# Gated linear attention in fp32 instead of three split passes, with its decay windows folded into zeros and a new order of steps

## The chip, the cores and the metric

One Trainium2 chip, one of its cores. The metric is the time of the whole kernel in device microseconds; lower is better. Engines: TensorE (PE, with its weight loads as PEld), VectorE (DVE), ScalarE (ACT), GpSimd (POOL), SyncE (SP).

## What is computed

Input x is 16 sequences of 256 tokens with 256 features, fp32. Four blocks follow each other, each with a residual: causal softmax attention with 16 heads, a gated FFN whose weights come from splines, gated linear attention, and the same FFN again. The change touches the third:

```python
q = silu(x @ Wq.T) * K ** -0.5            # K = 16, x is the layer-normed input
k = sigmoid(x @ Wk.T)
g = log_sigmoid(-k)
S = exp(g_t)[:, None] * S + k_t[:, None] * v_t[None, :]   # v = x, for each token t
o_t = q_t @ S
go = o @ Wog.T + x @ Wig.T
out = rms_norm(o) * g_weight * go * sigmoid(go)
```

## The kernel before

X holds all 4096 tokens in SBUF as 32 tiles of 128 tokens. The stages run one behind the other: attention with one sequence per period (until about 380 us), FFN (eight pairs of sequences, to about 574 us), gated linear attention (one sequence n per period, to about 775 us), FFN. All instructions and semaphores are written by hand; each engine runs its own list in order, and the order inside a period of the linear attention stands in the `period` functions (TensorE L1172, ScalarE L1504, VectorE L1875, GpSimd L720).

The scan over tokens is turned into products. Decays of a sequence are cumulated within windows, q is multiplied by the cumulated decay from a reference token and k by that to it, `g_products` (L1122) multiplies k by q over 112 rows (seven groups of 16 features, each with its window), `g_masked` (L1848) sets the future to zero, and `g_output` (L1154) multiplies the result by the values. `g_values` (L1132) has already multiplied x by Wog, so that o and o @ Wog.T come out of one accumulation, onto which `g_gate_in` (L1143) has put x @ Wig.T.

Precision: TensorE runs its products in fp32r. Each operand is split into a high part (ScalarE copies it to an fp32r tile, names with `_hi`) and a low part (VectorE or GpSimd subtracts the high part from the original, `_lo`), and `mm3` (L404 to L408) adds three passes. So the trace has all such products on L406, L407 and L408; tiles tell them apart: `wqk` projections, `wog` values, `wig` gate, `am` output, `qk` products.

ScalarE: `g_norm` (L1440, normalised input of n+2), `g_high_turned` (L1432), `g_activate` (L1449: tanh, silu, tanh, k, decay), `g_high_qk` (L1464), `g_high_am` (L1469), `g_high_x` and `g_high_values` (L1438, L1474), `g_squares` (L1485), `g_gate` (L1491), `g_normalise` (L1498). VectorE: `g_scans` (L1832, L1833: forward and backward cumulated products), `g_decayed` (L1838 reciprocal, L1840, L1842), the low parts (L1825, L1846, L1857, L1861), `g_stats` (L1813 to L1820), `g_mean_square` (L1867). GpSimd: `g_windows` (L685 to L693: q, k and decays times their windows), `g_low_x` (L678), small powers (L672, L698), `g_residual` (L702, L706, L710).

Many work tiles lie in one tensor, so the trace names them all `spline`.

At the start of the kernel the weights are turned and split: high parts on ScalarE (L1234, L1239), low parts on VectorE (L1587, L1595); GpSimd builds spline factors (L593 to L605) once the second sequence is normalised (L1581, L610).

## Time and profile before

| | |
|---|---|
| median of 3 runs | 972.94 us (972.71 to 973.38) |
| profiled execution, whole | 969.64 us |
| its span, first to last instruction | 967.9 us |
| busy TensorE, weight loads | 840.5 us (87%), 721.2 (75%) |
| busy VectorE, ScalarE, GpSimd | 690.2 (71%), 544.0 (56%), 402.8 (42%) |
| mean granted TensorE clock | 0.951 of 2.4 GHz |

The page divides the span into 40 slices of 24.2 us and gives the busy share in tenths. A timeline row reads: start in us, duration in us, engine, line, operation, output <- inputs, shapes, count, and in brackets how long the engine stood idle before and whom it waited for. Starts of successive matmuls give their spacing; durations contain the pipeline and overlap. A group row reads: line, engine, operation, names, shapes, count | busy us, mean ns | idle before, with releasers.

### The profile page before, as it was taken

What the parts mean: (1) busy time and instruction counts of PE and PEld (TensorE: products, weight loads), DVE (VectorE), ACT (ScalarE), POOL (GpSimd) and SP (SyncE); (2) the same over time, 40 slices, a digit from 0 to 9 for tenths busy, and PEclk for the clock granted to TensorE, in tenths of its full rate; (3) what the DMA queues carried; (4) which work ended last, traced back from release to release, by engine and by line L of the source; (5) the groups of instructions that cost most, each with busy time, mean ns of one, the idle gap of its engine ahead of it and who ended that gap; (6) DMA issues with size and microseconds to landing.
All of it is one profiled execution on the core that took longest, in us unless ns stands there. A gap on an engine that the chain in (4) does not pass through costs nothing.

```text
span 967.9 us, 21849 instructions
## 1 busy us (share of the span) xinstructions
PE 840.5 (87%) x7444; PEld 721.2 (75%) x7444; DVE 690.2 (71%) x1317; ACT 544.0 (56%) x1064; POOL 402.8 (42%) x465
## 2 busy tenths in 40 slices
PE   4599899999999977899999997877777569999997
PEld 4477677777777755788888887776676558888887
DVE  7567777777778763677776668888889536776765
ACT  3156455554555544666666655666665346666664
POOL 3922223222232242222223327899998543233220
PEclk9689999999999997999999998899999779999999
DMA  5946756667566530000000000000000000000001
GB/s 178 118 77 89 133 82 97 90 96 96 84 95 83 84 63 19 17 1 1 0 0 2 1 1 1 1 0 0 0 0 1 1 1 23 24 22 22 22 24 44
DMA packets 33752, 41.00 MB, mean 42 GB/s; under 512 B 4319, under 2 KB 25216, under 8 KB 33648
## 3 DMA queue, kind: packets, MB, share of 16 engines
q1 hardware_dynamic: 33690, 40.20, 25.0%
q8 instruction: 36, 0.59, 0.3%
q14 instruction: 26, 0.21, 0.1%
HBM read 9.25 MB, written 5.24 MB: 15 GB/s over the span
## 4 chain that ended last, share of the span: by engine, by line
PE 37%; DVE 26%; ACT 14%; issue 12%; POOL 4%; SPq 2%; DMA 2%; DVEq 1%; ACTq 1%; POOLq 0%
DVE inter L1771 6%; PE bank L406 5%; PE pair_a L840 5%; PE bank L408 4%; PE bank L407 4%; ACT stk L1389 4%; ACT gact L1394 4%; PE bank L854 3%; PE bank L1040 3%; PE pair_b L809 3%; DVE spline L1838 3%; DVE am_lo L1857 2%; DVE in_lo L1776 2%; DVE st L1745 2%; PE bank L867 2%
## 5 line engine op out<-in xcount | busy, mean ns | idle before, releaser
L583 POOL TENSOR_SCALAR_AFFINE_SELECT prob<-prob 128x512 f32<-128x512 f32 x128 | 82.0, 641 | 213.7 <-ACT prob L1265 213.7
L1265 ACT ACTIVATE prob<-pair_a 128x768 f32<-128x768 f32 x128 | 103.6, 809 | 96.1 <-PE pair_a L840 95.0
L1776 DVE TENSOR_TENSOR in_lo<-inter,in_hi 128x512 fp32r<-128x512 f32 x128 | 98.8, 772 | 78.7 <-ACT in_hi L1402 78.1
L406 PE MATMUL bank<-wd_hi,in_hi 128*128 128x256 f32 x512 | 147.4, 288 | 8.1 <-DVE X L1782 6.6
L408 PE MATMUL bank<-wd_hi,in_lo 128*128 128x256 f32 x512 | 142.9, 279 | 0.0
L407 PE MATMUL bank<-wd_lo,in_hi 128*128 128x256 f32 x512 | 142.6, 279 | 0.0
L1402 ACT ACTIVATE in_hi<-inter 128x512 fp32r<-128x512 f32 x128 | 80.9, 632 | 95.1 <-DVE inter L1771 95.1
L1618 DVE TENSOR_REDUCE mx<-pair_b 128x6 f32<-128x768 f32 x124 | 118.1, 952 | 18.6 <-PE pair_b L821 16.9
L1771 DVE TENSOR_TENSOR inter<-gact,pair_b 128x512 f32<-128x512 f32 x128 | 87.6, 684 | 49.6 <-ACT gact L1394 43.7
L406 PEld LDWEIGHTS bank<-wd_hi,in_hi 128*128 128x128 f32 x512 | 96.7, 189 | 16.3 <-issue 5.8
L407 PEld LDWEIGHTS bank<-wd_lo,in_hi 128*128 128x128 f32 x512 | 97.1, 190 | 3.6
L408 PEld LDWEIGHTS bank<-wd_hi,in_lo 128*128 128x128 f32 x512 | 96.7, 189 | 0.0
L1050 PE MATMUL bank<-ident,xe 128*126 128x128 f32 x512 | 82.8, 286 | 12.5 <-POOL xe L654 7.6
L1389 ACT ACTIVATE stk<-bank 126x512 fp32r<-126x512 f32 x128 | 75.0, 586 | 18.2 <-PE bank L1050 18.2
L646 POOL COPY xe<-xr 128x448 f32<-128x448 f32 x32 | 24.7, 771 | 138.9 <-ACT xe L1371 138.9
L1394 ACT ACTIVATE gact<-pair_a 128x512 f32<-128x512 f32 x128 | 75.9, 593 | 0.0
L1050 PEld LDWEIGHTS bank<-ident,xe 128*126 128x126 f32 x512 | 59.3, 145 | 22.2 <-ACT stk L1389 11.6
L840 PE MATMUL pair_a<-stack 50*128 50x256 f32 x512 | 65.9, 336 | 10.7 <-DMA stack<-mrow 7.6
L840 PEld LDWEIGHTS pair_a<-stack 50*128 50x128 f32 x512 | 39.3, 190 | 34.6 <-issue 18.3
L1076 PE MATMUL pair_a<-stk,cst 126*128 126x512 f32 x128 | 63.0, 492 | 0.5 <-ACT stk L1389 0.5
L809 PE MATMUL pair_b<-stack 48*128 48x256 f32 x496 | 54.2, 297 | 5.0 <-DVE stage L1609 3.6
L1079 PE MATMUL pair_b<-stk,cst 126*128 126x512 f32 x128 | 51.7, 404 | 0.0
(242 smaller groups left out, 2340.8 us busy)
## 6 DMA issues: line engine op xcount, KB each, us to landing
stack<-stage SPq DMA_DIRECT2D x192, 128.0 KB, 4.7
result<-X SPq DMA_DIRECT2D x8, 512.0 KB, 2.9
X<-in_attn_a_x SPq DMA_DIRECT2D x14, 256.0 KB, 5.0
stack<-mrow SPq DMA_DIRECT2D x128, 4.0 KB
wdx<-spline SPq DMA_DIRECT2D x1, 1024.0 KB
wd_lo<-wdx SPq DMA_DIRECT2D x16, 64.0 KB
spline<-factor_basis SPq DMA_DIRECT2D x1, 1008.0 KB, 6.8
win<-decay_windows SPq DMA_DIRECT2D x1, 672.0 KB, 7.5
```

What stands on the lines that cost most here:

```text
L406: pe.matmul(dst, l_hi, r_hi, start=first, stop=False)
L407: pe.matmul(dst, l_hi, r_lo, start=False, stop=False)
L408: return pe.matmul(dst, l_lo, r_hi, start=False, stop=last)
L809: pe.matmul(dst[:, n, at_col:at_col + S], stack[rows, u, h, p % PR, 0, P * t:P * t + P], stack[rows, u, h, p % PR, 1, :], start=(t == 1), ...
L840: i = pe.matmul(pair_a[:, n, at_col:at_col + S], stack[rows, u, h, p % PR, 1, P * t:P * t + P], stack[rows, u, h, p % PR, 0, :], start=Tru ...
L1050: i = pe.transpose(bank_t[0:NFX, P * t:P * t + P], xe[:, u, t, m].rearrange("p c f -> p (c f)").bitcast(F32), ident[:, :])
L1265: act.activation(prob[:, p % 4], pair_a[:, :, P:4 * P], ACT.Exp, scale=DK ** -0.5).then_inc(a_e, 1)
L1389: act.activation(stk[:, m % 2, :], bank_t[0:NFX, :], ACT.Copy).then_inc(f_.st, 1)
L1394: act.activation(gact[:, m % 2, :], pair_a[:, m % 2, :], ACT.Silu).then_inc(f_.si, 1)
L1618: dve.tensor_reduce(mx[:, h, :, p % PR, :], src[:, :, 0:3 * P].rearrange("p n (t k) -> p n t k", t=3), AX.X, ALU.max).then_inc(a_mx, 1)
L1771: dve.tensor_tensor(inter[:, m % 2, :], gact[:, m % 2, :], pair_b[:, m % 2, :], ALU.mult).then_inc(f_.up, 1)
L1776: dve.tensor_tensor(in_lo[:, m % LAG, :], inter[:, m % 2, :], in_hi[:, m % LAG, :].bitcast(F32), ALU.subtract).then_inc(f_.il, 1)
```

## The change

All products of the linear attention are single fp32 matmuls on unsplit tiles; the high copies stay as plain fp32 copies (ScalarE), the low parts are gone. `g_high_qk`, `g_high_am`, `g_low_qk`, `g_low_am`, `g_low_values`, `g_low_turned`, `g_low_x` and `g_windows` are gone. There are five groups of 16 rows instead of seven, in 112 rows with two gaps that are zero: three cross groups (rows 0 to 47) and two near groups (64 and 96), each for one half of every 128 tokens. Windows are bounded by zeros that GpSimd sets once in `dec` and `fk`; the decay is written in three pieces. The products skip the block above the diagonal. q, k and decays have two buffers. On TensorE the projections of n+1 move behind output, gate and turn, the values of n+1 behind the products of n; on ScalarE the activations of n+1 move from the third place to nearly the last; on VectorE the statistics move ahead of the scans.

```diff
-NG = 7
-GR = NG * KG
+GROUPS = (0, 16, 32, 64, 96)
+CROSS = 48
+NEAR = (64, 96)
+GR = 112
+AM = 3 * P
...
+def decay_starts():
+
+    w = np.zeros((GR, 2, S), np.float32)
+    for g, ref in ((0, 64), (1, 192), (2, 128)):
         r = slice(KG * g, KG * g + KG)
-        run[r] = 1.0
...
+        w[r, 0, ref] = 1.0
+        w[r, 1, ref - 1] = 1.0
+    for h in range(2):
+        w[NEAR[h]:NEAR[h] + KG, 0, 64 * h::P] = GROW
...
-        wog = sb("wog_hi", [P, CT, D], F32R), sb("wog_lo", [P, CT, D], F32R)
-        wig = sb("wig_hi", [P, CT, D], F32R), sb("wig_lo", [P, CT, D], F32R)
-        wqk_hi = sb("wqk_hi", [P, 2, CT, GR], F32R)
-        wqk_lo = sb("wqk_lo", [P, 2, CT, GR], F32R)
+        wog = sb("wog", [P, CT, D], F32)
+        wig = sb("wig", [P, CT, D], F32)
+        wqk = sb("wqk", [P, 2, CT, GR], F32)
...
-        qs, kt, ks, dt, dec, qwn, kwn, dq, dk, fq, fk = (gwork(1, GR)[:, 0] for _ in range(11))
+        am = am.rearrange("p t k -> p (t k)")[:, 0:AM]
+        qs, ks, dec = (gwork(2, GR) for _ in range(3))
+        kt, dt, fq, fk = (gwork(1, GR)[:, 0] for _ in range(4))
...
-            def g_low_x(n, u):
...
             def g_project(n, u):
 
-                pe.wait_ge(g_.xl, upto(g_.xl, n, 1))
+                pe.wait_ge(g_.xh, upto(g_.xh, n, 1))
                 pe.wait_ge(g_.qs, upto(g_.qs, n - 1, 1))
                 pe.wait_ge(g_.kt, upto(g_.kt, n - 1, 1))
                 for w in range(2):
                     for c in range(CT):
-                        i = mm3(pe, bank_p[0:GR, S * w:S * w + S], wqk_hi[:, w, c, :], wqk_lo[:, w, c, :],
-                                gT_hi[:, u, c, :], gT_lo[:, u, c, :], c == 0, c == CT - 1)
+                        i = pe.matmul(bank_p[0:GR, S * w:S * w + S], wqk[:, w, c, :], gT[:, u, c, :], start=c == 0,
+                                      stop=c == CT - 1)
                 i.then_inc(g_.qk, 1)
...
             def g_products(n):
 
-                pe.wait_ge(g_.qkl, upto(g_.qkl, n, 1))
+                pe.wait_ge(g_.kd, upto(g_.kd, n, 1))
+                pe.wait_ge(g_.qd, upto(g_.qd, n, 1))
                 pe.wait_ge(g_.am, upto(g_.am, n - 1, 1))
-                for t in range(TB):
-                    keys = slice(P * t, P * t + P)
-                    i = mm3(pe, pair_a[:, 0, S * t:S * t + S], qk_hi[:, 1, keys], qk_lo[:, 1, keys],
-                            qk_hi[:, 0, :], qk_lo[:, 0, :], True, True)
+                for at, rows, k, q in ((0, GR, 0, 0), (P, CROSS, 0, 1), (2 * P, GR, 1, 1)):
+                    k, q = slice(P * k, P * k + P), slice(P * q, P * q + P)
+                    i = pe.matmul(pair_a[:, 0, at:at + P], qk[0:rows, 1, k], qk[0:rows, 0, q], start=True, stop=True)
                 i.then_inc(g_.ap, 1)
...
             def g_values(n, u):
 
-                pe.wait_ge(g_.xl, upto(g_.xl, n, 1))
-                pe.wait_ge(g_.wl, upto(g_.wl, n - 1, 1))
+                pe.wait_ge(g_.xh, upto(g_.xh, n, 1))
+                pe.wait_ge(g_.wh, upto(g_.wh, n - 1, 1))
                 for t in range(TB):
                     for c in range(CT):
                         tok = slice(P * t, P * t + P)
-                        i = mm3(pe, pair_a[:, 1, D * t:D * t + D], gT_hi[:, u, c, tok], gT_lo[:, u, c, tok],
-                                wog[0][:, c, :], wog[1][:, c, :], c == 0, c == CT - 1)
+                        i = pe.matmul(pair_a[:, 1, D * t:D * t + D], gT[:, u, c, tok], wog[:, c, :], start=c == 0,
+                                      stop=c == CT - 1)
                 i.then_inc(g_.xw, 1)
...
             def g_output(n, u):
 
-                pe.wait_ge(g_.gl, upto(g_.gl, n, 1))
-                pe.wait_ge(g_.wl, upto(g_.wl, n, 1))
-                pe.wait_ge(g_.aml, upto(g_.aml, n, 1))
+                pe.wait_ge(g_.gh, upto(g_.gh, n, 1))
+                pe.wait_ge(g_.wh, upto(g_.wh, n, 1))
+                pe.wait_ge(g_.am, upto(g_.am, n, 1))
                 for q in range(TB):
-                    tok = slice(P * q, P * q + P)
                     for part in range(2):
                         cols = slice(D * part, D * part + D)
                         for t in range(q + 1):
-                            i = mm3(pe, out_bank(u, q)[:, cols], am_hi[:, t, tok], am_lo[:, t, tok],
-                                    val_hi[:, u, t, cols], val_lo[:, u, t, cols], False, part == 1 and t == q)
+                            tok = slice(P * (q + t), P * (q + t) + P)
+                            i = pe.matmul(out_bank(u, q)[:, cols], am[:, tok], val[:, u, t, cols], start=False,
+                                          stop=part == 1 and t == q)
                     i.then_inc(g_.o, 1)
...
                 pe.wait_ge(f_.res, upto(f_.res, PAIRS - 1, 2))
 
                 def period(n, u, prev2=True, prev=True, cur=True, nxt=True, nxt2=True, nxt3=True):
-                    if nxt:
-                        g_project(n + 1, 1 - u)
-                        g_values(n + 1, 1 - u)
                     if not cur:
                         f2_turn(0, 0, 0, bank_t)
                         f2_turn(0, 0, 1, bank_p)
...
                         g_gate_in(n, u)
                     if nxt2:
                         g_turn(n + 2, u)
+                    if nxt:
+                        g_project(n + 1, 1 - u)
                     if cur:
                         g_products(n)
+                    if nxt:
+                        g_values(n + 1, 1 - u)
 
                 run_gla(pe, period)
...
-            def g_activate(n):
+            def g_activate(n, u):
 
                 act.wait_ge(g_.qk, upto(g_.qk, n, 1))
-                act.wait_ge(g_.w, upto(g_.w, n - 1, 4))
+                act.wait_ge(g_.kd, upto(g_.kd, n - 2, 1))
                 act.activation(kt, bank_p[0:GR, S:2 * S], ACT.Tanh, scale=0.5).then_inc(g_.kt, 1)
-                act.activation(qs, bank_p[0:GR, 0:S], ACT.Silu).then_inc(g_.qs, 1)
+                act.activation(qs[:, u], bank_p[0:GR, 0:S], ACT.Silu).then_inc(g_.qs, 1)
                 act.wait_ge(g_.kt, upto(g_.kt, n, 1))
                 act.activation(dt, kt, ACT.Tanh, bias=quarter[0:GR, :], scale=0.25).then_inc(g_.dt, 1)
-                act.activation(ks, kt, ACT.Copy, bias=0.5, scale=0.5).then_inc(g_.ks, 1)
+                act.activation(ks[:, u], kt, ACT.Copy, bias=0.5 * KG ** -0.5, scale=0.5 * KG ** -0.5).then_inc(g_.ks, 1)
                 act.wait_ge(g_.dt, upto(g_.dt, n, 1))
-                act.activation(dec, dt, ACT.Copy, bias=0.5, scale=-0.5).then_inc(g_.de, 1)
...
+                for rows, cut in (((0, 32), P), ((32, CROSS), 0), ((NEAR[0], GR), 64)):
+                    to, of = dec[rows[0]:rows[1], u], dt[rows[0]:rows[1]]
+                    if cut:
+                        to, of = (v.rearrange("p (w s) -> p w s", s=cut)[:, :, 1:] for v in (to, of))
+                    i = act.activation(to, of, ACT.Copy, bias=0.5, scale=-0.5)
+                i.then_inc(g_.de, 1)
...
-                    if prev:
-                        g_high_am(n - 1)
                     if prev2:
                         g_normalise(n - 2, u)
                     if not cur:
...
                         f2_store_turned(0, bank_t)
                     if nxt2:
                         g_norm(n + 2, u)
-                    if nxt:
-                        g_activate(n + 1)
-                    if cur:
-                        g_high_qk(n)
                     if prev:
                         g_squares(n - 1, 1 - u)
-                    if nxt:
-                        g_high_x(n + 1, 1 - u)
-                        g_high_values(n + 1, 1 - u)
                     if nxt2:
                         g_high_turned(n + 2, u)
                     if prev:
                         g_gate(n - 1, 1 - u)
+                    if nxt:
+                        g_high_x(n + 1, 1 - u)
+                        g_activate(n + 1, 1 - u)
+                        g_high_values(n + 1, 1 - u)
...
-            def low_gla_weights():
...
+            def clear_gaps():
+                for gap in (CROSS, NEAR[0] + KG):
+                    i = dve.memset(wqk[:, :, :, gap:gap + KG], 0.0)
...
-            low_weights(4)
-            low_weights(5)
-            low_gla_weights()
+            clear_gaps()
...
-            def g_scans(n):
...
+            def g_scans(n, u):
+
+                dve.wait_ge(g_.de, upto(g_.de, n, 1))
+                dve.wait_ge(g_.kd, upto(g_.kd, n - 1, 1))
+                dve.tensor_tensor_scan(fq, dec[:, u], win[:, 0], 0.0, ALU.mult, ALU.add).then_inc(g_.sf, 1)
+                dve.tensor_tensor_scan(fk[0:CROSS, S - 2::-1], win[0:CROSS, 1, S - 2::-1], dec[0:CROSS, u, S - 1:0:-1],
+                                       0.0, ALU.add, ALU.mult).then_inc(g_.sb, 1)
+
+            def g_decayed(n, u):
                 dve.wait_ge(g_.sf, upto(g_.sf, n, 1))
-                dve.reciprocal(fk[0:64], fq[0:64]).then_inc(g_.rc, 1)
-                dve.wait_ge(g_.qkh, upto(g_.qkh, n - 1, 1))
-                dve.tensor_tensor(qk[:, 0], qwn, fq, ALU.mult).then_inc(g_.qd, 1)
+                for h in range(2):
+                    near = slice(NEAR[h], NEAR[h] + KG)
+                    f, t = (v[near].rearrange("p (t h s) -> p h t s", h=2, s=64)[:, h] for v in (fk, fq))
+                    i = dve.reciprocal(f, t)
+                i.then_inc(g_.rc, 1)
+                dve.wait_ge(g_.qs, upto(g_.qs, n, 1))
+                dve.wait_ge(g_.ap, upto(g_.ap, n - 1, 1))
+                dve.tensor_tensor(qk[:, 0], qs[:, u], fq, ALU.mult).then_inc(g_.qd, 1)
+                dve.wait_ge(g_.sb, upto(g_.sb, n, 1))
+                dve.wait_ge(g_.ks, upto(g_.ks, n, 1))
                 dve.wait_ge(g_.rc, upto(g_.rc, n, 1))
-                dve.tensor_tensor(qk[:, 1], kwn, fk, ALU.mult).then_inc(g_.kd, 1)
...
+                dve.tensor_tensor(qk[:, 1], ks[:, u], fk, ALU.mult).then_inc(g_.kd, 1)
...
+                dve.wait_ge(g_.o, upto(g_.o, n - 1, 2))
+                dve.scalar_tensor_tensor(out=am, in0=pair_a[:, 0, 0:AM], scalar=BIG, in1=causal01[:, :], op0=ALU.min,
+                                         op1=ALU.mult).then_inc(g_.am, 1)
...
                     if prev:
                         g_masked(n - 1)
-                    if cur:
-                        g_scans(n)
-                    if prev:
-                        g_low_am(n - 1)
                     if nxt3:
                         g_stats(n + 3, 1 - u)
                     if cur:
-                        g_decayed(n)
-                        g_low_qk(n)
+                        g_scans(n, u)
+                        g_decayed(n, u)
                     if prev:
                         g_mean_square(n - 1)
-                    if nxt:
-                        g_low_values(n + 1, 1 - u)
-                    if nxt2:
-                        g_low_turned(n + 2, u)
```

## Rows read from the trace of the kernel before

**Rows 1.** Table by stage: stretch, length, busy PE, PEld, DVE, ACT, POOL, clock, DMA

```profile
583.00:595.00 12.00, 11.02 (x70) 11.00 (x70) 10.36 (x19) 7.38 (x20) 7.61 (x10) 0.72 0.01 2
...
643.00:655.00 12.00, 8.45 (x65) 7.86 (x66) 10.27 (x18) 7.39 (x20) 10.71 (x13) 0.99 0.00 0
```

**Rows 2.** Timeline, TensorE: first products, pass after pass, turns, projections, last products

```profile
583.98 0.58 PE L406 MATMUL pair_a<-qk_hi 112*128 112x256 f32 x1 [3.24 <-DVE qk_lo L1846]
...
613.24 0.28 PE L407 MATMUL pair_b<-val_lo,am_hi 128*128 128x256 f32 x1
...
613.36 0.28 PE L408 MATMUL pair_b<-val_hi,am_lo 128*128 128x256 f32 x1
...
615.61 0.60 PE L1107 MATMUL bank<-ident,spline 128*128 128x128 f32 x4
...
619.59 0.34 PE L406 MATMUL bank<-gT_hi,wqk_hi 128*112 128x256 f32 x1 [1.72 <-DVE gT_lo L1825]
...
758.30 0.28 PE L406 MATMUL pair_a<-qk_hi 112*128 112x256 f32 x1
```

**Rows 3.** Chain of waits in order of time, inside one period

```profile
610.20 1.63 DVE am_lo L1857
```

**Rows 4.** Timeline: first scan with GpSimd at rest; a GpSimd product with VectorE at rest

```profile
576.99 0.68 DVE L1832 TENSOR_TENSOR_SCAN spline<-spline,win 112x256 f32<-112x256 f32 x1
...
774.78 1.26 POOL L702 TENSOR_TENSOR spline<-spline,gw_row 128x512 f32<-128x512 f32 x1 [4.84 <-ACT spline L1498]
```

**Rows 5.** True fp32 matmuls and 512 columns: timeline rows, then durations min/median/max

```profile
260.28 0.64 PE L854 MATMUL bank<-prob,V 128*32 128x256 f32 x8
260.74 0.40 PE L858 MATMUL bank<-prob,V 128*32 128x128 f32 x8
...
443.41 2.02 PE L1040 MATMUL bank<-mom,xf 128*128 128x128 f32 x16 [0.20 <-DVE xf L1765]
...
L854 PE MATMUL bank<-prob,V x512: 378/402/635, 53.7 to 375.7; 128*32 128x256 f32 x171
...
L1076 PE MATMUL pair_a<-stk,cst x128: 401/480/776, 385.1 to 957.9; 126*128 126x512 f32 x128
```

**Rows 6.** Groups by line and shape, VectorE, 585 to 740 us

```profile
L1838 DVE RECIPROCAL spline<-spline 64x256 f32<-64x256 f32 x13 | 22.6, 1737 | 0.0
L1857 DVE TENSOR_TENSOR am_lo<-spline,am_hi 128x512 fp32r<-128x512 f32 x14 | 21.6, 1544 | 0.4
L1832 DVE TENSOR_TENSOR_SCAN spline<-spline,win 112x256 f32<-112x256 f32 x14 | 18.7, 1337 | 0.0
L1846 DVE TENSOR_TENSOR qk_lo<-spline,qk_hi 112x512 fp32r<-112x512 f32 x13 | 10.3, 790 | 9.1 <-ACT qk_hi L1464 9.1
...
L1825 DVE TENSOR_TENSOR gT_lo<-bank,gT_hi 128x512 fp32r<-128x512 f32 x14 | 9.5, 679 | 0.0
```

**Rows 7.** Groups by line and shape, ScalarE, 560 to 780 us

```profile
L1464 ACT ACTIVATE qk_hi<-spline 112x512 fp32r<-112x512 f32 x16 | 10.1, 632 | 53.6 <-DVE spline L1842 53.6
...
L1459 ACT ACTIVATE spline<-spline 112x256 f32<-112x256 f32 x16 | 6.7, 417 | 0.0
```

**Rows 8.** Timeline at the edges: residual of FFN, values of 0, squares of 15

```profile
573.56 1.37 DVE L1782 TENSOR_TENSOR X<-bank,X 128x512 f32<-128x512 f32 x2 [1.06 <-PE bank L408]
...
574.04 0.28 PE L406 MATMUL pair_a<-wog_hi,gT_hi 128*128 128x256 f32 x1
...
764.40 0.38 ACT L1485 ACTIVATE junk<-bank 128x256 f32<-128x256 f32 x1 [0.78 <-PE bank L408]
```

**Rows 9.** Start of the kernel: two rows of the chain, then two of the timeline

```profile
16.90 0.68 DVE wog_lo L1587
...
18.18 0.92 DVE wqk_lo L1595 x7
...
46.09 0.35 DVE L1575 TENSOR_SCALAR ve<-mv 128x2 f32<-128x2 f32 x1
...
46.52 0.71 POOL L577 TENSOR_TENSOR rs<-ve,half_neg 128x2 f32<-128x2 f32 x1
```

More of the change, by code:

```diff
@@ L1237, in _ @@
             turned = prep_bank[6][:, 0:4 * KG].rearrange("p (m k) -> p m k", k=KG)
-            for g in range(NG):
-                act.activation(wqk_hi[:, :, :, KG * g:KG * g + KG].rearrange("p n c k -> p (n c) k"), turned,
+            for g in GROUPS:
+                act.activation(wqk[:, :, :, g:g + KG].rearrange("p n c k -> p (n c) k"), turned,
                                ACT.Copy).then_inc(s_prep_hi, 1)
```

158 lines of the change are left out of this document (37 added, 121 removed).

## The prediction, made before the change was run

> **What bounds the kernel now.** I read the page's slices first. From slice 25 to slice 31 (581 to 750 us) TensorE is busy 7 to 8 tenths, where the slices before have 9, VectorE 8 to 9, GpSimd 7 to 9, and the DMA engines not at all. This is the gated linear attention, the only stage whose loop the change touches. The table by stage gives it in stretches of 12 us [rows 1]: TensorE 11.0 us busy where its granted clock is 0.72, 8.45 where it is 0.99; VectorE 10.3, ScalarE 7.4, GpSimd 7.6 to 10.7. Then the length of one sequence: the first product of sequence 0 starts at 583.98, that of sequence 15 at 758.30 [rows 2], so 174.32 us for 15 periods, 11.62 each. TensorE's own work does not need that: a pass of 256 columns follows the last after 0.12 us [rows 2], and a period has 60 (projections 12, values 12, output 18, gate 12, products 6) and four transposes (about 0.45 us, from the row of 0.60 us with its drain): 60 x 0.118 + 0.45 = 7.5 us. The rest is waiting, such as the 1.72 us before the projections, for VectorE's low part of the turned input [rows 2]. The chain of waits runs in this stage through VectorE, with the low part of the masked products (1.63 us) as a link in each period [rows 3]. So VectorE with its hand-overs to ScalarE bounds this stage, and GpSimd lengthens it: the first scan takes 0.68 us in the period in which GpSimd rests, and 1.34 in the mean of the later ones, where GpSimd works on two SBUF operands at the same time [rows 4, 6].
>
> **TensorE, the price of full precision.** 54 of the 60 passes become 18 single fp32 matmuls with 256 columns (projections 4, values 4, gate 4, output 6). An fp32 matmul appears in the trace as two records. What a record of 256 columns costs is shown nearest by the attention stage: 4 matmuls on four column strips, 8 records, occupy 0.46 us from start to start [rows 5]. If the strips run beside each other, as their separate array columns allow, that is two records of 0.23. The duration speaks for this too: a record lasts 378 to 402 ns, where an fp32r pass of 256 columns lasts 280 and the shortest one of 512 columns 401 [rows 2, 5]; an fp32 record lasts like a pass of twice its columns. So 0.22 to 0.23 per record, 0.45 us per matmul. The lower bound is the moments' matmul with 128 columns: 16 records in 2.02 us, 0.116 each, which could be the cadence of weight loads and then hold for 256 columns too: 0.23 per matmul. The upper bound is 0.46. I take 0.45.
>
> The Trainium skill ("FP8 and Floating Point Precision", TensorE Precision Notes) says that true fp32 needs four passes through the array; that is 0.43 to 0.47 us by the 0.12 of a pass, and the row of 0.46 agrees. The same skill ("Perfetto Trace Analysis", the table of what 100% means) halves the rate for FP32_LOW_HIGH; taken as the price of the whole matmul that gives 0.23, the cheap rival below.
>
> The 6 passes of the products become 3 matmuls of 128 columns, 6 records of 0.116: 0.70 us, as now. The transposes stay. TensorE then needs per period 18 x 0.45 + 0.70 + 0.45 = **9.25 us**, against 7.5.
>
> **What VectorE, ScalarE and GpSimd lose.** VectorE loses the low parts of masked products, q/k, values and turned input: 1.54 + 0.79 + 0.68 + 0.68 = 3.69 us by their group means [rows 6] (the values' row is like that of the turned input), and a quarter of the masking (an estimate of 0.15 us, by its columns). The first scan (mean 1.34 against 0.68 undisturbed) should lose part of its wait, since GpSimd's window products and low values are gone. The reciprocal keeps its elements per lane: 256 columns in one instruction become two of 128, 1.74 us together plus one start. VectorE: 10.3 - 3.7 - 0.15 = 6.4 us [rows 1, 6]. ScalarE loses two roundings of 0.63 us and gets three decay writes for one of 0.42: 7.4 - 1.26 + 0.84 = 7.0 [rows 1, 7]. GpSimd loses five of nine large products and is nobody's bound by busy time. TensorE becomes the bound if the loops fit into 9.25 us.
>
> **The new order, against 9.25 us.** TensorE's order becomes output of n-1 (0 to 2.70), gate of n (to 4.50), turn of n+2 (4.95), projections of n+1 (6.75), products of n (7.45), values of n+1 (9.25). The loop that carries through VectorE is products of n, masking, statistics, scans of n+1, reciprocals, q and k products, products of n+1: 0.70 + VectorE's 6.4 + about 0.5 of hand-overs = 7.6 us. It fits with 1.6 to spare. The masking (done about 0.8 us after the products) lies beside the 1.80 us of values, which is what moving these behind the products gives; so the output no longer waits. What moving the projections costs: ScalarE's tanh and silu start at about 7.0, the decays are ready at about 9.5, 0.3 us into the next period, while VectorE is still in the statistics. Behind the activations in ScalarE's queue wait only the copy of the values (ready at 9.5 as well) and, next, the normalising of n-1, which the gate of n+1 needs by 2.70 of the next period and gets at about 1.7. The new waits on the copies of ScalarE replace waits on later VectorE steps, so nothing gets later by them. The two buffers for q, k and decays cost nothing; the one more memset on GpSimd lies in the first FFN, where the page shows it idle for 138.9 us.
>
> **Edges of the stage.** The values of sequence 0 start at 574.04 [rows 8]. By the new order: values 1.8, gate 1.8, a turn that must wait for ScalarE until about 577.75 and takes 0.45, projections 1.8: products at about 580.0; by VectorE (its residual of the first FFN ends at 574.9 [rows 8], then 5.3 us of its chain) 580.3. I take 580.3, against 583.98. Then 13 periods of 9.25, one without the turn (8.8), one without turn and projections (7.0): 580.3 + 120.25 + 8.8 + 7.0 = 716.35, against 758.30: **-41.95 us**. Until ScalarE squares the last output it is now 764.40 - 758.30 = 6.1 us [rows 2, 8]; later 0.70 + 0.90 of transposes + 2.70 + 0.2 of drain, 4.5 to 4.6: -1.5. The first projection inside the first FFN is 0.35 us longer and its decay writes 0.8; against that GpSimd no longer collides with VectorE there: 0.
>
> **The start of the kernel.** In the chain of waits stand three low parts of weights that the change drops, from 16.90 to 19.10: 2.2 us [rows 9]. They delay GpSimd's factor work. But this ends together with a second chain: VectorE's own statistics end at 46.44, and GpSimd's next step begins at 46.52 [rows 9]. That second chain moves by only 0.25 us (its first copy waits for TensorE). So 0.25, not 1.8.
>
> **Sum.** 41.95 + 1.5 + 0.25 = 43.7 us off a span of 967.9 (profiled execution 969.64), so a span of 924.2. The median of the three runs, 972.94, is 3.3 above the profiled execution; I carry the difference over: 972.94 - 43.7 = **929.2 us**. From 0.44 to 0.46 per matmul with transitions the period is 9.05 to 9.6, the time 926 to 934; with 1 us for the edges 925 to 935.
>
> **Rivals.**
> 1. A wait takes TensorE's place (19%): VectorE's scans and q/k products read two SBUF operands, as did the instructions that took longer in [rows 3, 6], and GpSimd still runs three products of 1.26 us each per period [rows 4]. For: the first scan's mean is twice its undisturbed time. Against: with a slack of 1.6 us one such wait is swallowed. With two or more on the loop it is 7.6 + 2 x 1.3 = 10.2 us per period: +0.95 x 14 = 13, so 942. The Trainium skill ("SBUF — State Buffer", two separate sides) calls the shared port an exclusive lock for the whole instruction, also for VectorE with two SBUF inputs; the rows agree.
> 2. The fp32 record costs what 128 columns do, 0.23 per matmul (8%). TensorE would need 5.3 us, and ScalarE with its waits, about 8.4, would bound: -0.85 x 14, so 917. Against: the durations.
> 3. The clock (9%). It was 0.72 in the stretch after TensorE had stood idle 3.24 us before the first product, and 0.99 in another [rows 1, 2]. If some idling remains and it is granted about 0.88, the period is 10.5: 947. Against: TensorE has no wait left in my plan.
> 4. Slower than before (4%): fp32 records keep TensorE on the 1.2 GHz level through most of the stage. At half the clock a period costs twice 9.25, so 18.5 us: +9.25 x 14.5 = 134, so 1063. It decides from a period of 9.25 + 43.7 / 14.5 = 12.3, a mean granted clock of 9.25 / 12.3 = 0.75. Against: the moments' fp32 records run at 0.112 to 0.116 inside a full-clock stretch; but these last only 2 us.
>
> **Chances.** The forecast 60%. The range takes in rival 1 and most of rival 3 and leaves out rivals 2 and 4: 921 to 946. Faster by over 0.2% 0.95, within 0.2% (about what a measurement of this kernel can tell from no change) 0.01, slower 0.04.
>
> **What would show it.** After: products of 0 and 15 start 136 us apart; fp32 matmuls of 256 columns come every 0.45 us; TensorE is over 95% busy in the stage at a granted clock of 0.97 or more, while VectorE is at 6 to 7 us per 9.25; no row of TensorE waits for VectorE over 0.2 us in the inner periods; the second FFN keeps its 193 us. The prediction fails if a gap stays before the products each period (rival 1), if the spacing is 0.23 (rival 2), or if the granted clock is below 0.95 (rivals 3 and 4).

## The result, and the profile after

The changed kernel takes 933.79 us (median; 931.85 to 938.12), the kernel before 972.83 beside it: a ratio of 0.9619, 95% interval 0.9594 to 0.9644. So 39.0 us less, where 43.7 were forecast. The profiled execution took 931.85 with a span of 930.1, against 969.64 and 967.9.

The page, three rows of it: busy time by engine, TensorE in 40 slices, and its granted clock.

```profile
PE 845.3 (91%) x7156; PEld 712.4 (77%) x7156; DVE 642.3 (69%) x1262; ACT 543.8 (58%) x1062; POOL 324.6 (35%) x386
...
PE   4599899999999996699999999999999499999997
...
PEclk9689999999999999899999999999999689999999
```

TensorE's slices of the stage (26 to 31, 581 to 721 us; a slice is now 23.25 us) show 9, where there were 7 and 8. The table by stage (columns as in [rows 1]) says it sharply:

```profile
590.00:640.00 50.00, 50.00 (x251) 42.90 (x250) 38.22 (x74) 38.86 (x106) 27.21 (x29) 1.00 0.00 0
640.00:700.00 60.00, 60.00 (x299) 51.44 (x299) 46.78 (x88) 48.37 (x131) 34.22 (x40) 1.00 0.00 1
```

50.00 of 50.00 us and 60.00 of 60.00 busy, at a granted clock of 1.00 (2.4 GHz), against 8.45 of 12 at 0.99 in [rows 1]. VectorE is busy 7.1 to 7.2 us per period (38.22 / 50 x 9.27), ScalarE 7.2 to 7.5, GpSimd 5.0 to 5.3. In the kernel before, the granted clock over the same two stretches was 0.90 and 0.94. From the third period on each took about 11.8 us, in stretches with a clock of 0.81 as in those with 0.96. So the shorter period isn't a gift of the clock.

TensorE's timeline: the first products, one inner period, the last products. A row with x8 is eight records in sequence, so a group's cost is read from its start to the next start:

```profile
584.12 1.32 PE L1094 MATMUL pair_a<-spline 112*128 112x128 f32 x6 [0.47 <-DVE spline L1793]
...
639.81 1.22 PE L1094 MATMUL pair_a<-spline 112*128 112x128 f32 x6
640.87 1.89 PE L1104 MATMUL pair_a<-wog,gT 128*128 128x256 f32 x8
642.60 2.75 PE L1129 MATMUL pair_b<-val,spline 128*128 128x256 f32 x12
645.19 1.89 PE L1115 MATMUL bank<-wig,gT 128*128 128x256 f32 x8
646.92 0.60 PE L1072 MATMUL bank<-ident,spline 128*128 128x128 f32 x4
647.35 1.89 PE L1083 MATMUL bank<-gT,wqk 128*112 128x256 f32 x8
649.08 1.22 PE L1094 MATMUL pair_a<-spline 112*128 112x128 f32 x6
...
721.34 1.32 PE L1094 MATMUL pair_a<-spline 112*128 112x128 f32 x6 [0.38 <-DVE spline L1793]
```

Products 1.06, values 1.73, output 2.59, gate 1.73, turn 0.43, projections 1.73: 9.27 us per period, and no bracket (no wait) inside it. Against [rows 2], where the projections waited 1.72 us, nothing waits. From the products of sequence 0 to those of sequence 15 are 137.22 us, against 174.32.

VectorE in the same period, with two products of GpSimd's residual that lie beside its steps:

```profile
636.94 1.12 DVE L1789 TENSOR_TENSOR spline<-spline 112x256 f32<-112x256 f32 x1
637.98 0.41 DVE L1793 TENSOR_TENSOR spline<-spline 112x256 f32<-112x256 f32 x1
638.32 1.24 DVE L1805 TENSOR_SCALAR vs<-ssq 128x2 f32<-128x2 f32 x1
641.07 0.56 DVE L1799 SCALAR_TENSOR_TENSOR spline<-pair_a,causal 128x384 f32<-128x384 f32 x1 [1.51 <-PE pair_a L1094]
...
642.88 0.68 DVE L1776 TENSOR_TENSOR_SCAN spline<-spline,win 112x256 f32<-112x256 f32 x1
...
636.51 1.27 POOL L676 TENSOR_TENSOR spline<-spline 128x512 f32<-128x512 f32 x1 [0.16 <-POOL spline L672]
638.07 1.46 POOL L680 TENSOR_TENSOR X<-X,spline 128x512 f32 x1 [0.29 <-POOL spline L676]
```

The k product ends at 638.39, TensorE takes it up at 639.81: VectorE is 1.42 us ahead. The low parts of [rows 3, 6] are gone, the first scan takes 0.68 as in [rows 4], and VectorE now waits for TensorE.

Where the 37.8 us of the two profiled spans lie, by the same landmarks in both traces (the first is the moments' matmul after the attention stage, 397.67 before and 402.52 after):

| part | forecast | measured |
|---|---|---|
| up to that landmark | -0.25 | +4.85 |
| from it to the products of sequence 0 | -3.68 | -4.71 (186.31 to 181.60) |
| products of 0 to products of 15 | -38.27 | -37.10 (174.32 to 137.22) |
| from there to the end | -1.5 | -0.84 (209.60 to 208.76) |
| sum | -43.7 | -37.8 |

### The profile page after: what moved, and what is told of

Its sections match the earlier page's. It is cut to its first block, busy times and chain, and to the rows that moved or that the text cites. A ratio compares the mean times of both kernels' runs of the same rounds, so it can differ in the third digit from the quotient of the medians.

```text
span 930.1 us, 21031 instructions
## 1 busy us (share of the span) xinstructions
PE 845.3 (91%) x7156; PEld 712.4 (77%) x7156; DVE 642.3 (69%) x1262; ACT 543.8 (58%) x1062; POOL 324.6 (35%) x386
## 4 chain that ended last, share of the span: by engine, by line
PE 56%; DVE 15%; ACT 12%; issue 9%; DMA 3%; SPq 3%; POOL 2%; ACTq 1%; DVEq 1%; POOLq 0%
PE bank L394 6%; DVE inter L1721 5%; PE bank L395 5%; PE bank L396 5%; PE pair_a L804 5%; ACT stk L1355 4%; ACT gact L1360 4%; PE bank L818 4%; PE pair_b L773 3%; PE bank L1005 3%; PE pair_a L1104 3%; PE bank L1083 3%; PE bank L1015 2%; PE bank L1129 2%; PE pair_b L1129 2%
## 5 line engine op out<-in xcount | busy, mean ns | idle before, releaser
L1231 ACT ACTIVATE prob<-pair_a 128x768 f32<-128x768 f32 x128 | 103.6, 810 | 95.0 <-PE pair_a L804 93.9
L1355 ACT ACTIVATE stk<-bank 126x512 fp32r<-126x512 f32 x128 | 75.1, 587 | 17.5 <-PE bank L1015 17.4
```

The source lines that it names most:

```text
L1231: act.activation(prob[:, p % 4], pair_a[:, :, P:4 * P], ACT.Exp, scale=DK ** -0.5).then_inc(a_e, 1)
L1355: act.activation(stk[:, m % 2, :], bank_t[0:NFX, :], ACT.Copy).then_inc(f_.st, 1)
```

## Experiments: is it TensorE?

Theory A: TensorE's own work is the period; the loop through VectorE has a slack (time to spare in each period) near 1.5 us. Three kernels load or unload one side.

**Values multiplied twice** (L1101 of the changed kernel; the second pass of the loop writes the same results):

```
-                for t in range(TB):
+                for t in (0, 1, 0, 1):
```

> The changed kernel with the values product computed twice: 4 more fp32 matmuls of 256 columns per sequence, same result. If TensorE's work is the bound, each costs its full 0.44 us: 16 x 1.76 = 28 us, so 962. If another engine or a loop of waits also bounds the period, part of it is swallowed: under 950.

Measured 960.3 us (959.13 to 961.15), ratio to before 0.9906 (0.9875 to 0.9936). TensorE's timeline:

```profile
643.91 3.62 PE L1104 MATMUL pair_a<-wog,gT 128*128 128x256 f32 x16
647.36 2.75 PE L1129 MATMUL bank<-val,spline 128*128 128x256 f32 x12
```

The values take 3.45 instead of 1.73, the period goes from 9.27 to 10.99: all of the 1.72 comes out, none is hidden. TensorE bounds the period.

**VectorE padded**: four copies of one bank ahead of the scans, used by nobody.

```
+                        for k in range(4):
+                            dve.tensor_copy(pad[:, k, :], pair_a[:, 0, :])
```

> The changed kernel, with four copies of one bank's 512 columns (about 0.69 us each by the values' and states' rows, 2.6 us together) put into each period on VectorE ahead of the scans; nothing uses them. Theory A (TensorE bounds the loop, VectorE's part has about 1.4 us to spare): the first 1.4 us of the pad are absorbed, the rest comes out as period, 9.27 + 1.2 = 10.4 to 10.6 us, the whole 950 to 956 us. Theory B (VectorE wholly off the path): period 9.27, 933 us. Theory C (the loop has no slack, the two only happen to agree): period 11.9, 973 us.

Measured 961.64 us (959.59 to 963.68), ratio 0.9884 (0.9775 to 0.9993).

```profile
636.42 2.48 DVE L1820 COPY pad<-pair_a 128x512 f32<-128x512 f32 x4
...
639.41 1.69 DVE L1778 TENSOR_TENSOR_SCAN spline<-win,spline 48x255 f32<-48x255 f32 x1
...
655.25 1.32 PE L1095 MATMUL pair_a<-spline 112*128 112x128 f32 x6 [1.31 <-DVE spline L1794]
```

The pad takes 2.39 us from start to start. The products' starts at 644.41 and 655.25 are 10.84 apart, 1.57 more than 9.27. Theory B (VectorE irrelevant) and theory C (no slack, 11.9) both fall. The slack can be read from the same period. From the start of the products to the end of VectorE's k product are 10.79 us (644.41 to 655.20), where the changed kernel needs 7.84 (630.55 to 638.39). So 2.95 us were added and 1.38 of them absorbed, which is the 1.42 read above to within 0.04.

More than the pad was added because it moved VectorE's steps against GpSimd's: the second scan now begins inside a GpSimd product (638.86 to 640.56) and takes 1.69 us, 1.68 in the mean of 13 periods, against 0.66 in the changed kernel; the q product in turn takes 0.42 instead of 1.12. My 950 to 956 was too low by this collision, and because this execution reached the first landmark at 405.68, 3.2 us later than the changed kernel's.

TensorE's granted clock over 590 to 640 is 0.93 here instead of 1.00. By stretches of 10 us it is 0.83 over 590 to 600 and 630 to 640, and 1.00 between, where TensorE waits in each period just the same. The period across the second of these is 11.15 us instead of 10.84. With TensorE's old order alone (below), where it waits 2.2 us in each period, the clock is 1.00 over the same 50 us. So the waits by themselves do not explain the lower clock; its cause is open.

**Four matmuls less**: one contraction chunk instead of two in projections and values. This leaves out half of the input features of q, k, decays and values.

```
-                    for c in range(CT):
+                    for c in range(1):
```

> The changed kernel without the second half of the contraction in the projections and the values (4 fp32 matmuls of 256 columns fewer per sequence; q, k, decays and values are then those of half of the features). TensorE's work falls from 9.27 to 7.5 us a period. By the loop through VectorE read from the trace (products, masking, statistics, scans, reciprocals, q and k products: 7.85 us) the next bound is 7.9 to 8.3: 15 to 20 us less, 914 to 919. If TensorE alone counted: 26 us less, 908. If something else is already at the bound: under 8 us less, over 926.

Measured 922.99 us (922.98 and 923.0), ratio 0.9523 (0.9483 to 0.9563).

```profile
646.46 1.32 PE L1094 MATMUL pair_a<-spline 112*128 112x128 f32 x6
...
647.93 0.56 DVE L1799 SCALAR_TENSOR_TENSOR spline<-pair_a,causal 128x384 f32<-128x384 f32 x1 [0.36 <-PE pair_a L1094]
...
654.57 1.32 PE L1094 MATMUL pair_a<-spline 112*128 112x128 f32 x6
```

TensorE's work falls by 1.7 us, to 7.5, but most periods only to 8.0 to 8.1 (8.3 in the mean of all 15): VectorE waits 0.36 us instead of 1.51, and its k product ends 0.06 us before TensorE starts the products (654.51 and 654.57), so the loop is the next bound, at 8.0 to 8.1 where the prediction had 7.6. TensorE reads 49.79 of 50 us busy here as well (590 to 640), though it isn't the bound: the busy share alone doesn't tell the two cases apart, the added matmuls do. The time is above the expected 914 to 919 mainly because the profiled execution reached the moments of the first FFN at 407.79, 5.3 us later than the changed kernel's (what differs there: below, under the start).

## Experiments: what is the new order worth?

The prediction gave the order part of the gain: the masking would lie beside the values, "which is what moving these behind the products gives; so the output no longer waits".

**TensorE's old order alone**, everything else as changed:

```
                 def period(n, u, ...):
+                    if nxt:
+                        g_project(n + 1, 1 - u)
+                        g_values(n + 1, 1 - u)
...
-                    if nxt:
-                        g_project(n + 1, 1 - u)
                     if cur:
                         g_products(n)
-                    if nxt:
-                        g_values(n + 1, 1 - u)
```

> The changed kernel with TensorE's old order: projections and values of the next sequence first in each period, then output, gate, turn, products. TensorE's work stays 9.25 us a period. If TensorE's work alone bounds the stage, the time stays at about 933. If the order is what hides the masking and VectorE's chain: the masked products of n are now followed by 3.5 us of projections and values instead of 1.7, which is still enough, but the decays come earlier for ScalarE and the loop products, masking, scans, products keeps its 7.85 us, so 0 to 0.3 us a period, at most 938. The rival says that the old order brings a stall before the products of over 1 us a period: over 948.

Measured 967.02 us (964.66 to 972.01), ratio 0.997 (0.995 to 0.9991): nearly the whole gain is gone. That is over the 948 of the rival, but the stall isn't before the products, where the rival had it:

```profile
642.13 1.22 PE L1094 MATMUL pair_a<-spline 112*128 112x128 f32 x6
644.60 1.98 PE L1083 MATMUL bank<-gT,wqk 128*112 128x256 f32 x8 [1.25 <-ACT spline L1419]
647.12 1.97 PE L1104 MATMUL pair_a<-wog,gT 128*128 128x256 f32 x8 [0.54 <-ACT val L1434]
```

The waits are for ScalarE: the next projections overwrite the bank that its silu (L1419) still has to read, and the values the bank that it copies at L1434. From start to start they cost 1.41 and 0.79 us, which is 2.2 of the 2.27 by which the period grew, to 11.54. In this variant ScalarE kept the new order, in which the activations come last in its period. That suggested that the mismatch costs, and not the old order as such: none of my accounts had a wait for ScalarE.

**TensorE's and ScalarE's old orders together**, full precision kept: the same move in ScalarE's period (activate behind the normalising, copies of x and values behind the squares).

> The changed kernel with the old order on TensorE and on ScalarE (activations third, turned input and gate last); fp32 products, zeros and two buffers stay. e4 had the old order on TensorE alone, and TensorE then waited 1.25 us a period for ScalarE's silu and 0.54 for its copy of the values. Theory A (each of the two orders is as good as the other as long as both engines have the same; TensorE's 9.27 us of work bounds the stage): 9.3 to 9.5 us a period, 934 to 938. Theory B (the new order itself carries a large part of the gain): 10.5 us or more a period, over 950.

Measured 931.62 us (931.13 to 935.72), ratio 0.9624 (0.9585 to 0.9664).

```profile
641.05 1.22 PE L1094 MATMUL pair_a<-spline 112*128 112x128 f32 x6
...
650.31 1.22 PE L1094 MATMUL pair_a<-spline 112*128 112x128 f32 x6
```

9.26 us from products to products, without a wait: the same time as the changed kernel. Theory A holds. Here projections and values (3.5 us) stand between products and output, so the masking is hidden just as well. Once the four low parts are gone, the new order of these two engines gives nothing that can be measured; what matters here is that the two have the same one. VectorE kept its new order (statistics ahead of the scans) in both runs; what that gives was not tried.

**The new orders without full precision**: the kernel before, with TensorE's and ScalarE's new orders and VectorE's low part of the values moved behind that of the turned input. ScalarE's rounding of q and k, which the changed kernel no longer has, had to be given a place too: behind the rounding of the turned input.

> The kernel before, still split in high and low parts, with the changed kernel's order on TensorE and ScalarE and VectorE's matching place for the values' low part; precision as before. If the new order is what shortened the period (theory B): under 955 us. If the order is worth nothing without full precision (theory A): no gain, 968 to 1000 us, since the masked scores' low part still stands between VectorE's product and the output.

Measured 1045.57 us (1045.54 and 1045.61), ratio 1.0747 (1.0641 to 1.0852).

```profile
641.19 0.55 PE L406 MATMUL bank<-val_hi,am_hi 128*128 128x256 f32 x1 [5.92 <-DVE am_lo L1857]
...
652.61 0.69 DVE L1861 TENSOR_TENSOR val_lo<-pair_a,val_hi 128x512 fp32r<-128x512 f32 x1 [2.44 <-ACT val_hi L1475]
...
654.53 2.80 DVE L1833 TENSOR_TENSOR_SCAN spline<-spline,win 48x256 f32<-48x256 f32 x1
657.36 1.57 DVE L1857 TENSOR_TENSOR am_lo<-spline,am_hi 128x512 fp32r<-128x512 f32 x1
```

That is 73 us slower than before, much more than the 1000 us at which I had put the end. VectorE's queue holds the reason: the low part of the values must wait for values that TensorE now makes after the products; the masking is queued behind it, then both scans, then the low part of the masked products, and TensorE waits for that, 5.92 us in the period whose output stands in the first row. Earlier in the period of the last rows VectorE also stands idle 4.17 us for ScalarE's rounding of q and k (L1846 at 648.80). So the order alone doesn't bring the gain. How much of the 73 us belongs to the order itself and how much to the place that I chose for that rounding isn't separated. It also shows that the same order on TensorE and ScalarE isn't enough: VectorE's queue has to match as well.

## Experiments: the start of the kernel

**The changed kernel once more**, to have its spread:

> The changed kernel once more, beside the kernel before on the same chip. The first trace of it had the linear attention 15 periods of 9.15 us from first to last products (137.2 us, as forecast) but reached the first FFN's second moments at 402.5 us instead of 397.7. Theory A (the start of the kernel became slower by its own change): the same landmark lies at 402 to 403 again, span 928 to 934. Theory B (the start wanders from execution to execution, whatever the kernel): the landmark moves by 2 us or more in either direction.

Measured 933.96 us (930.57 to 937.05), ratio 0.9629 (0.96 to 0.9658). The landmark lies at 403.52, 1.0 us later than the first time: the shift is there again, as theory A had it.

**The nine subtractions put back** on VectorE at the start, results unused:

```
             low_xT(0, 0, False)
+            spare_lows()
             clear_gaps()
```

> The changed kernel with the nine VectorE subtractions at the start put back (results unused), so that GpSimd's factor work begins as late as before. Theory A (GpSimd's earlier factor work collides with VectorE's copy of the maxima, 2.33 us instead of 0.75, and TensorE falls to the 1.2 GHz level earlier): 4 to 5 us faster than the changed kernel, median about 929, landmark near 398. Theory B (start wanders): within 1 us of the changed kernel. Theory C (the removed work was on the chain of waits, as the chain's rows said): 2 us slower.

**The same subtractions moved later in the kernel before**, behind the second normalising:

```
             low_xT(0, 0, False)
+            normalise(1, 1)
+            low_qk(0, 0)
             low_weights(4)
             low_weights(5)
             low_gla_weights()
-            normalise(1, 1)
-            low_qk(0, 0)
```

> The kernel before with the same nine subtractions kept, but moved behind the normalising of the second sequence, so that GpSimd starts its factor work early as in the changed kernel. Theory A: 3 to 5 us slower than the kernel before, about 977. Theory B: no difference beyond 1 us. Theory C: up to 2 us faster.

Measured 930.4 us (928.93 to 932.94; ratio 0.9585, 0.9561 to 0.961) and 971.9 us (968.32 to 975.37; ratio 1.0006, 0.9984 to 1.0028). So the work that was taken away costs nothing when it is put back; the median even falls by 3.6 us against the changed kernel beside it, with intervals that just overlap. Moving the same work in the kernel before gives no difference that can be measured, where theory A wanted 3 to 5 us.

The landmarks go against theory A too. With the subtractions back the profiled execution reached the moments at 402.43, not near 398. It was the slowest of the six (932.94), so the faster ones have no trace. The kernel before with the work moved reached them at 401.15, 3.5 us later than before, though its median is only 1.3 us above the 970.57 of the kernel before beside it. So the collision below is a fact of the traces, but what it costs at the end of the kernel isn't shown.

The traces show why the 2.2 us taken away bring nothing at the start. Rows of the changed kernel (GpSimd, VectorE, GpSimd), then of the one with the subtractions back:

```profile
34.63 4.18 POOL L581 TENSOR_TENSOR spline<-spline,cpw 128x2016 f32<-128x2016 f32 x1 [0.17 <-POOL cx L589]
...
36.51 2.33 DVE L1577 COPY mx<-mx 128x8 f32<-128x8 f32 x1
...
48.91 0.71 POOL L565 TENSOR_TENSOR rs<-ve,half_neg 128x2 f32<-128x2 f32 x1 [4.17 <-DVE ve L1532]
```

```profile
36.93 0.72 DVE L1589 COPY mx<-mx 128x8 f32<-128x8 f32 x1
...
37.80 4.22 POOL L582 TENSOR_TENSOR spline<-spline,cpw 128x2016 f32<-128x2016 f32 x1 [0.17 <-POOL cx L590]
```

GpSimd's factor work does start 2.1 us earlier (17.73 against 19.82), so its third large product lies at 34.63 to 38.81 instead of starting at 36.66. VectorE's copy of 8 columns begins inside it and ends at 38.84, together with it. Where the copy comes a few tenths ahead of that product, it is through before it begins (at 37.65 with the product at 37.80 above; at 36.53 with 36.66 in the trace of before). The changed kernel once more shows it again (product to 39.26, a copy of 3.03 us to 39.29). The sharpest case is the mixed version below:

```profile
37.07 4.17 POOL L584 TENSOR_TENSOR spline<-spline,cpw 128x2016 f32<-128x2016 f32 x1 [0.17 <-POOL cx L592]
...
37.15 4.12 DVE L1587 COPY mx<-mx 128x8 f32<-128x8 f32 x1
```

It comes 0.08 us too late and takes 4.12 us. So GpSimd's gain is lost on VectorE's second chain, for which GpSimd then stands idle (4.17 us): its next step is at 48.91, where it was at 46.52 [rows 9].

That is 2.4 us, but they aren't simply half of the 4.85. The attention stage has 128 exponentials on ScalarE (L1265 before, L1231 after), which serve as landmarks. Their starts:

| | before | changed | subtractions back |
|---|---|---|---|
| 1st | 45.51 | 48.19 | 46.64 |
| 17th | 92.28 | 93.75 | 94.88 |
| 33rd | 134.37 | 138.09 | 138.67 |
| 113th | 336.04 | 339.78 | 340.39 |
| 121st | 354.68 | 357.31 | 358.93 |
| moments | 397.67 | 402.52 | 402.43 |

Of the 2.7 us at the first one the changed kernel has 1.5 left at the 17th. It loses 2.25 between the 17th and the 33rd, nothing up to the 113th, wins back 1.1 up to the 121st, and loses 2.2 behind it. Both later losses go with a wait of TensorE for a transfer of the maxima (before, then after):

```profile
102.77 0.50 PE L840 MATMUL pair_a<-stack 50*128 50x256 f32 x4 [1.44 <-DMA stack<-mrow]
...
364.78 0.80 PE L840 MATMUL pair_a<-stack 50*128 50x256 f32 x4 [3.34 <-DMA stack<-mrow]
```

```profile
104.97 0.50 PE L804 MATMUL pair_a<-stack 50*128 50x256 f32 x4 [2.18 <-DMA stack<-mrow]
...
369.62 0.80 PE L804 MATMUL pair_a<-stack 50*128 50x256 f32 x4 [5.55 <-DMA stack<-mrow]
```

The first wait is 0.74 us longer. Behind it TensorE's passes come every 0.21 us instead of 0.12 for about 4 us, which is its 1.2 GHz level: the granted clock is 0.57 over 105 to 109 us, and 0.91 over 95 to 115, where it was 1.00 before. The kernel with the subtractions back has the same slow passes and 0.91 too; its better start was gone already at the 17th exponential. With TensorE's old order alone the wait is 2.18 as well and the clock stays at 1.00, so the wait doesn't decide it by itself.

The second wait was 3.0 to 3.7 us in the three traces of kernels with the old linear attention, and 3.3 to 8.2 in the nine with the new one (3.8 with the subtractions back, 3.3 with all old orders, 6.8 with four matmuls less, 8.2 with VectorE padded), though most of these edits don't touch this stage. The causes of both waits and of the slow passes are open. The executions of one kernel lie up to 8 us apart, and one trace for each kernel can't tell what part of the 4.85 us belongs to the change.

## Experiment: a version ahead of both

If full precision costs 0.43 us per matmul and three split passes cost 0.354 (3 x 0.118), the matmuls whose low parts are cheap should be split, and those whose low parts stand on the loop (masked products, q and k) should not. So: the changed kernel, with projections, values and gate as three passes on high and low halves of the turned input and the weights; products and output in full precision.

```
-                        i = pe.matmul(bank_p[0:GR, S * w:S * w + S], wqk[:, w, c, :], gT[:, u, c, :], ...
+                        i = mm3(pe, bank_p[0:GR, S * w:S * w + S], wqk[:, w, c, :], wqk_lo[:, w, c, :],
+                                gT[:, u, c, :], gT_lo[:, u, c, :], c == 0, c == CT - 1)
...
+                    if nxt2:
+                        g_low_turned(n + 2, u)
```

> A version that may beat both: projections, values and gate again as three fp32r passes each (0.354 us instead of 0.44), products and output in fp32, new order, zeros and two buffers kept; it needs the low part of the turned input (0.68 us of VectorE, placed where VectorE waits for the products) and the three low parts of weights at the start. TensorE 9.27 - 12 x 0.086 = 8.2 us a period. If the loop through VectorE stays at 7.85, the period is 8.2 to 8.5: 12 to 16 us less than the changed kernel, and up to 4 us less from the start as in e2: 915 to 922. If VectorE's extra step lands on the loop: 8.9 us or more, over 926.

Measured 919.68 us (917.88 to 921.35), ratio to before 0.9483 (0.9448 to 0.9517): 14 us ahead of the changed kernel. That is inside the expected 915 to 922. Products of its sequences 1 and 2, then VectorE:

```profile
593.12 1.22 PE L1097 MATMUL pair_a<-spline 112*128 112x128 f32 x6
601.46 1.22 PE L1097 MATMUL pair_a<-spline 112*128 112x128 f32 x6
...
643.53 0.68 DVE L1787 TENSOR_TENSOR gT_lo<-bank,gT_hi 128x512 fp32r<-128x512 f32 x1
644.51 0.56 DVE L1817 SCALAR_TENSOR_TENSOR spline<-pair_a,causal 128x384 f32<-128x384 f32 x1 [0.30 <-PE pair_a L1097]
```

Most periods are 8.34 us: 12 matmuls at 0.076 less, 0.9 in all. The one low part that is left (0.68 us) fits into VectorE's wait for the products, of which 0.30 us remain here; in the next period nothing remains. TensorE and the loop are now nearly balanced.

## Why the prediction was right, and where it was not

**The bound and its change.** Right. VectorE's loop bounded the stage, it was freed, and TensorE's work became the period. Both signs of it were seen: TensorE 100% busy at a clock of 1.00, and, which decides it, 1.72 us more work giving 1.72 us more period. What freed VectorE isn't taken apart: the change removes VectorE's low parts and GpSimd's window products together, folds the windows into zeros, and doubles buffers, and no run puts windows, buffers or a low part back alone. The mixed version shows only that full precision in projections, values and gate wasn't needed for the gain, and that one low part (0.68 us) could have stayed.

**The price of a full-precision matmul.** Forecast 0.45 us for 256 columns, measured 1.73 / 4 = 0.43. The two bounds were far apart (0.23 and 0.46), and taking the row that had the same duration per record decided it. The Trainium skill ("FP8 and Floating Point Precision", TensorE Precision Notes) counts four passes for true fp32; by the 0.118 us of a pass that is 0.47, so the trace agrees to within a tenth. (The prediction gave 0.43 to 0.47 for it; from the passes of this trace only the 0.47 follows.) The halved rate that the same skill gives for FP32_LOW_HIGH ("Perfetto Trace Analysis", the table of what 100% means) would have given 0.23 if it were the price of the whole matmul; here it isn't.

**The products.** This term was mis-sized: 0.70 forecast, 1.06 measured. I took the cadence of 0.116 per record from the moments' matmul [rows 5]. Three of the six records, read in narrow windows (the count is that of the window):

```profile
640.13 0.79 PE L1094 MATMUL pair_a<-spline 48*128 48x128 f32 x3
...
640.34 0.69 PE L1094 MATMUL pair_a<-spline 48*128 48x128 f32 x3
...
640.54 0.49 PE L1094 MATMUL pair_a<-spline 112*128 112x128 f32 x2
```

The records start at 639.81, 639.93, 640.13, 640.34, 640.54, 640.76, and the values at 640.87: the first and the last step are 0.11 to 0.12, the four between them 0.20 to 0.22. Why the longer ones stand here and not among the moments was not tried. This error (+0.36) and those of the 18 matmuls (18 x 0.018 = -0.32) and the turn (-0.02) cancel almost: 9.27 against 9.25. That the period came out this close is luck: two errors of a third of a microsecond met.

**VectorE and its slack.** Forecast 6.4 us busy and a loop of 7.6; measured 7.1 to 7.2 busy, and 7.84 for the loop in the changed kernel (8.0 to 8.1 in the run with four matmuls less). The 6.4 itself was summed wrongly: 10.3 is VectorE's time in a stretch of 12 us, which is 9.95 in a period of 11.62, so the sum should have read 6.1. What was missed is the collision with GpSimd, as rival 1 had it: the q product takes 1.12 us where the k product of the same shape takes 0.41, and the mean square of 2 columns 1.24 where it takes 0.16 in the padded kernel's mean. Only the q product stands on the loop, and the slack swallowed it, as said there. The Trainium skill ("SBUF — State Buffer", two separate sides) calls the port that the two share an exclusive lock for the whole instruction; the trace agrees: the q product begins at 636.94 inside a GpSimd product that ends at 637.78 and ends 0.28 us behind that, the mean square begins at 638.32 inside one that ends at 639.53 and ends 0.03 us behind that.

**The order.** The step that failed in the reasoning, without harm to the number: I gave the new order the merit for hiding the masking. With TensorE and ScalarE both in the old order the time is the same (931.62 against 933.79).

**The end of the stage.** Forecast -1.5 until the squares of the last output, measured nothing (rows of VectorE, TensorE and ScalarE):

```profile
721.21 1.26 DVE L1805 TENSOR_SCALAR vs<-ssq 128x2 f32<-128x2 f32 x1
722.39 1.37 DVE L1708 TENSOR_SCALAR xr<-X,mv,rs 128x256 f32<-128x256 f32 x4
...
723.81 1.09 PE L994 MATMUL bank<-ident,xr 128*128 128x128 f32 x8 [1.15 <-DVE xr L1708]
...
727.53 0.38 ACT L1446 ACTIVATE junk<-bank 128x256 f32<-128x256 f32 x1 [0.55 <-PE bank L1129]
```

The squares start 6.19 us after the products of 15 (721.34), as before (6.10). Here there is no slack, so a collision with GpSimd (the mean square takes 1.26 us) delays the second FFN's normalised input, and TensorE waits 1.15 us for it; the products add the 0.4 us they were mis-sized by. Another collision just ahead (the k product at 719.80 takes 1.49 us) delays the products of 15 themselves and is part of their period of 7.74 us, where 7.0 were forecast. The -0.84 of the table was gained behind this point, where I expected nothing.

**The first FFN and the way into the stage.** Forecast -3.68, measured -4.71, of which 3.1 between the first projections (562.67 before, 565.92 after) and the products of sequence 0, and 1.6 ahead of that, unexplained. TensorE also met a wait of 1.50 us there (for ScalarE's L1355 at 571.59), which I had put at nothing.

**The start of the kernel.** The step that failed in size and sign: -0.25 forecast, +4.85 in the profiled pair. I checked which chain ends last, but not what the earlier GpSimd work would collide with. GpSimd's next step comes 2.4 us late through that collision, but the rest of the 4.85 arises at two places of the attention stage that the change doesn't touch, and what makes them longer stays open. By the medians putting the work back gives 3.6 us, an amount at the edge of what the runs can tell, and its trace doesn't show it.

By the profiled pair the shortfall against the forecast is this part and little else: the stage itself and its edges gave 42.65 of 43.45.

## What to carry to other kernels

Precision has two prices: passes on TensorE, and the low parts that another engine must make in between. Where those low parts stand on a loop, full precision (0.43 us instead of 0.354) can be the faster choice; the fastest version here chose matmul by matmul. Give engines that hand work to each other the same order before asking which order is better; and when work is removed from a queue, look at what then starts earlier on GpSimd and what short VectorE instruction it will meet.

## What was not expected of the hardware

A VectorE copy of 8 columns began inside a GpSimd product of 4.2 us in nine of the twelve traces. It took 2.32 to 4.12 us there and ended each time 0.02 to 0.03 us after that product; in the other three it began 0.28 to 0.88 us ahead of the product and took 0.17 to 0.75. The price of such a collision is what is left of the GpSimd instruction, and in this kernel 0.36 us (from 0.28 ahead to 0.08 behind) lie between nothing and 4 us. And TensorE's granted clock held 1.00 through 110 us at full load with full-precision records. It was also 1.00 over 590 to 640 us where TensorE waited 2.2 us in each period (its old order alone), and 0.93 where padded VectorE made it wait 1.3 us.
